# A fused attention + spiking-MLP layer: a sixth buffer for attention weights over the query/key planes, two pairs of value runs joined, and the places of an interval laid out anew

## The reference

```
xn = layernorm(x)
q, k, v = xn Wq + bq, xn Wk + bk, xn Wv + bv        # 16 heads of 16 features
q, k    = rotary(q), rotary(k)
attn    = softmax(causal(q k^T / 4)) v,  then  attn Wo + bo
h       = relu(xn W_fc)^2                            # 1024 features
y       = h W_proj                                   # 256 features
spikes  = 5 steps of: mem = 0.9 mem + y - (mem > 1); count (mem > 1);  count / 5
out     = x + attn part + spikes
```

## Time and profile before

| | us |
|---|---|
| runs, median of 3 | 2201.42 (2200.13 to 2207.49) |
| profiled execution | 2198.7 |
| its span, first to last instruction | 2196.9 |
| TensorE busy | 2093.1 (95% of the span) |
| ScalarE busy | 1451.5 (66%) |
| VectorE busy | 1403.9 (64%) |
| GpSimd busy | 1125.3 (51%) |

### The profile page before, as it was taken

How to read it: one execution, slowest core, us unless ns; L and a number is a source line. 1 busy time by engine, 2 the same in 40 slices (tenths; PEclk the granted TensorE clock), 3 DMA queues, 4 the chain that set the end, 5 groups by cost and what they waited for, 6 DMA issues and landing times.

```text
span 2196.9 us, 67675 instructions
## 1 busy us (share of the span) xinstructions
PE 2093.1 (95%) x25492; PEld 1502.4 (68%) x25492; DVE 1403.9 (64%) x2139; ACT 1451.5 (66%) x1676; POOL 1125.3 (51%) x1072
## 2 busy tenths in 40 slices
PE   5899999999999999999999999999999999999995
PEld 4667676767767677676767767677676766767663
DVE  7566585766758576585666757576585666757443
ACT  3666667666676766667666676766667667676662
POOL 5455473545646355463555646455463554636341
PEclk9999999999999999999999999999999999999997
DMA  5353635455364453635445364453635445364442
GB/s 198 118 157 87 192 104 156 138 118 181 93 183 112 127 173 87 197 104 151 143 116 179 94 177 116 127 175 86 199 104 150 144 111 180 97 172 120 111 113 70
DMA packets 169866, 299.97 MB, mean 137 GB/s; under 512 B 25104, under 2 KB 114960, under 8 KB 157200
## 3 DMA queue, kind: packets, MB, share of 16 engines
q1 hardware_dynamic: 169616, 296.10, 47.3%
HBM read 174.89 MB, written 103.28 MB: 127 GB/s over the span
## 4 chain that ended last, share of the span: by engine, by line
PE 64%; issue 11%; POOL 9%; DMA 6%; DVE 5%; ACT 3%; SPq 0%; POOLq 0%; DVEq 0%; ACTq 0%
PE pair L1525 17%; PE pair L1322 13%; PE pair L1508 10%; PE pair L1331 10%; PE pair L1300 6%; PE pair L1248 5%; DMA recip_rows<-recip_dram 4%; POOL probs L691 4%; POOL h_lo L683 3%; ACT probs L808 3%; PE pair L1314 2%; POOL rs L669 1%; DMA recip_dram<-denom 1%; DVE rs L1087 1%; DVE h_sq L1065 1%
## 5 line engine op out<-in xcount | busy, mean ns | idle before, releaser
L808 ACT ACTIVATE probs<-pair 128x1024 f32<-128x1024 f32 x1152 | 1146.2, 1029 | 552.9 <-PE pair L1508 552.0
L683 POOL TENSOR_TENSOR h_lo<-h_sq,h_hi 128x512 fp32r<-128x512 f32 x256 | 399.1, 1559 | 451.1 <-DVE h_hi L1067 450.7
L1331 PE MATMUL pair<-wproj_hi,h_hi 64*128 64x256 f32 x2048 | 584.8, 286 | 0.0
L691 POOL TENSOR_SCALAR_AFFINE_SELECT probs<-probs 128x512 f32<-128x512 f32 x512 | 395.3, 789 | 367.9 <-ACT probs L808 366.6
L1331 PE MATMUL pair<-wproj_hi,h_lo 64*128 64x256 f32 x2048 | 572.1, 279 | 0.0
L1331 PE MATMUL pair<-wproj_lo,h_hi 64*128 64x256 f32 x2048 | 571.7, 279 | 0.0
L1322 PE MATMUL pair<-xT_hi,wfc_hi 64*128 64x256 f32 x2048 | 546.6, 285 | 19.5 <-DVE y_sb L1094 8.2
L1525 PE MATMUL pair<-probs,v_sb 128*17 128x512 f32 (+3 forms) x6144 | 548.3, 488 | 13.3 <-POOL probs L691 12.5
L1322 PE MATMUL pair<-xT_lo,wfc_hi 64*128 64x256 f32 x2048 | 535.2, 279 | 0.0
L1322 PE MATMUL pair<-xT_hi,wfc_lo 64*128 64x256 f32 x2048 | 534.8, 279 | 0.0
L1508 PE MATMUL pair<-q_ring,k_ring 64*128 64x512 f32 (+3 forms) x3072 | 448.5, 359 | 18.3 <-ACT probs L808 14.6
(11 more groups left out here) (113 smaller groups left out, 2888.9 us busy)
## 6 DMA issues: line engine op xcount, KB each, us to landing
q_ring<-qk_dram SPq DMA_DIRECT2D x384, 128.0 KB
k_ring<-qk_dram SPq DMA_DIRECT2D x384, 128.0 KB
qk_dram<-planes SPq DMA_DIRECT2D x64, 512.0 KB, 2.8
qk_dram<-rot_b SPq DMA_DIRECT2D x62, 512.0 KB, 3.7
xn<-in_x SPq DMA_DIRECT2D x16, 1024.0 KB, 5.9
rs<-in_x SPq DMA_DIRECT2D x64, 256.0 KB, 2.9
acc_dram<-rs SPq DMA_DIRECT2D x64, 256.0 KB, 4.5
attn<-numer SPq DMA_DIRECT2D x256, 64.0 KB, 2.3
```

Of the source, the lines that this page charges most:

```text
L683: pool.tensor_tensor(h_lo[i % HB][:, :], h_sq[i % HB][:, :], h_hi[i % HB][:, :].bitcast(F32), ALU.subtract).then_inc(h_lo_done, 1)
L691: ins = pool.affine_select(view, view, [[0, 4], [1, P]], ALU.is_ge, 0.0, base=0, channel_multiplier=-1)
L808: act.activation(probs[BUFFER[n]][:, 2 * pr:2 * pr + 2, :], pair[m % NSLOT][:, :, :], ACT.Exp, scale=SCALE).then_inc(exp_done, 1)
L1331: return pe.matmul(proj_bank[:, t * D:(t + 1) * D], h[rows, a * T2 + t * P:a * T2 + (t + 1) * P], w[rows, f, :], start=i % ITEMS_OF_GROUP ...
```

## The change

There is a sixth weight buffer for four units of the second half (21, 26, 30 and 35), laid over the two `planes`; ScalarE waits for the stores of all planes before unit 21, and for all value runs of the interval before it writes plane 0. Units 13 to 19, and others, get other buffers. The runs of steps 12 and 13 become one at step 13, those of steps 16 and 17 one at step 17, so there are 14 runs. Nearly every table of places is new. The number of operations of each kind is the same. Cut only by the tables `STATS_AT` and `XN_AT` (statistics and normalisation on VectorE, spread over more places) and by context:

```diff
...
-RUNS = {2: ((0, 0), (1, 0), (1, 1), (2, 0)), 3: ((3, 0), (4, 0)), 4: ((5, 0), (5, 1), (6, 0)), 5: ((7, 0), (8, 0), (2, 1)),
-        6: ((9, 0), (10, 0), (10, 1), (11, 0)), 7: ((12, 0), (13, 0)), 8: ((14, 0), (14, 1), (15, 0)),
-        9: ((16, 0), (17, 0), (11, 1))}
-RUN_AT = {n + h * NSTEP // 2: [(u + 2 * NU * h, seg) for u, seg in run] for h in range(2) for n, run in RUNS.items()}
+EARLY_RUNS = {2: ((0, 0), (1, 0), (1, 1), (2, 0)), 3: ((3, 0), (4, 0)), 4: ((5, 0), (5, 1), (6, 0)),
+              5: ((7, 0), (8, 0), (2, 1)), 6: ((9, 0), (10, 0), (10, 1), (11, 0)), 7: ((12, 0), (13, 0)),
+              8: ((14, 0), (14, 1), (15, 0)), 9: ((16, 0), (17, 0), (11, 1))}
+LATE_RUNS = {11: EARLY_RUNS[2], 13: EARLY_RUNS[3] + EARLY_RUNS[4], 14: EARLY_RUNS[5], 15: EARLY_RUNS[6],
+             17: EARLY_RUNS[7] + EARLY_RUNS[8], 18: EARLY_RUNS[9]}
+RUN_AT = {**EARLY_RUNS, **{n: tuple((u + NUNIT // 2, seg) for u, seg in run) for n, run in LATE_RUNS.items()}}
-BUFFER = (0, 1, 2, 3, 4, 0, 1, 3, 4, 0, 1, 2, 3, 0, 1, 0, 3, 0, 1, 0, 2, 3, 4, 0, 1, 3, 4, 0, 1, 2, 3, 0, 1, 0, 3, 1)
+BUFFER = (0, 1, 2, 3, 4, 0, 1, 3, 4, 0, 1, 2, 3, 4, 0, 1, 3, 4, 0, 1, 2, 5, 3, 4, 0, 1, 5, 0, 3, 4, 5, 1, 2, 0, 3, 5)
+LATE_UNITS = [n for n in range(NUNIT) if BUFFER[n] == NPB - 1]
...
-VALUES_AT = {(0, 0): ((0, 0),), (0, 3): ((0, 1), (1, 0)), (1, 0): ((1, 1),), (1, 3): ((2, 0),), (1, 4): ((2, 1),)}
-TAKE_V_AT = {(0, 3): (0,), (1, 0): (1,), (1, 4): (2, 3)}
+VALUES_AT = {(0, 0): ((0, 0),), (0, 2): ((0, 1),), (0, 4): ((1, 0),), (1, 0): ((1, 1),), (1, 3): ((2, 0),),
+             (1, 4): ((2, 1),)}
+TAKE_V_AT = {(0, 2): (0,), (1, 0): (1,), (1, 4): (2, 3)}
-QK_AT = {(2, 4): (0, 0), (3, 1): (0, 1), (3, 3): (1, 0), (4, 0): (1, 1), (4, 3): (2, 0), (5, 0): (2, 1),
+QK_AT = {(2, 4): (0, 0), (3, 0): (0, 1), (3, 3): (1, 0), (4, 0): (1, 1), (4, 3): (2, 0), (5, 0): (2, 1),
          (5, 3): (3, 0), (6, 0): (3, 1)}
-SUM_QK_AT = {(3, 2): 0, (4, 2): 1, (5, 2): 2, (6, 2): 3}
-PLANE_AT = {(3, 4): 0, (4, 4): 1, (5, 4): 2, (6, 4): 3}
-SQUARE_AT = {(4, 2): 0, (5, 2): 1, (6, 2): 2, (7, 2): 3}
+SUM_QK_AT = {(3, 2): 0, (4, 1): 1, (5, 2): 2, (5, 4): 3}
+PLANE_AT = {(3, 4): 0, (5, 0): 1, (6, 0): 2, (7, 2): 3}
+SQUARE_AT = {(3, 4): 0, (5, 3): 1, (6, 2): 2, (7, 1): 3}
...
-MLP_AT = {(6, 3): (0,), (7, 0): (1,), (7, 4): (2,), (8, 2): (3, 4), (8, 4): (5, 6), (9, 3): (7, 8), (10, 0): (9,),
-          (10, 3): (10,), (11, 0): (11, 12), (11, 3): (13, 14), (12, 0): (15,), (12, 3): (16,), (13, 0): (17,),
-          (13, 3): (18,), (14, 0): (19, 20), (14, 3): (21, 22), (15, 0): (23,), (15, 3): (24,),
-          (16, 0): (25,), (16, 3): (26,), (17, 0): (27, 28), (17, 3): (29,)}
+MLP_AT = {(6, 4): (0,), (7, 0): (1,), (7, 4): (2,), (8, 2): (3, 4), (8, 4): (5,), (9, 2): (6,), (9, 4): (7, 8),
+          (10, 1): (9,), (10, 4): (10,), (11, 0): (11,), (11, 3): (12,), (11, 4): (13,), (12, 0): (14,),
+          (12, 2): (15,), (12, 3): (16,), (13, 0): (17,), (13, 3): (18,), (14, 0): (19,), (14, 2): (20,),
+          (14, 4): (21,), (15, 0): (22,), (15, 3): (23, 24), (16, 0): (25,), (16, 3): (26,), (16, 4): (27,),
+          (17, 0): (28,), (17, 4): (29,)}
-Y_AT = {(10, 0): 0, (13, 0): 1, (16, 0): 2}
+Y_AT = {(10, 2): 0, (13, 0): 1, (16, 0): 2}
-Y_CARRIED_AT = (1, 0)
+Y_CARRIED_AT = (2, 1)
...
-RELU_AT = {**expanded_at(MLP_AT, NFC), (7, 0): (0,), (7, 3): (1,)}
+RELU_AT = {(7, 0): (0,), (7, 2): (1,), (8, 2): (2,), (9, 0): (3,), (9, 4): (4,), (10, 4): (5,), (11, 0): (6,),
+           (11, 4): (7,), (12, 4): (8,), (13, 1): (9,), (14, 1): (10,), (14, 4): (11,), (15, 3): (12,),
+           (16, 0): (13,), (16, 4): (14,), (17, 4): (15,)}
...
-SPIKES_HERE = {(8, 3): (0, 0), (8, 4): (0, 1), (9, 1): (0, 2), (9, 2): (0, 3), (9, 3): (0, 4), (9, 4): (0, 5),
-               (10, 2): (1, 0), (10, 3): (1, 1), (10, 4): (1, 2), (11, 1): (1, 3), (11, 2): (1, 4), (11, 3): (1, 5)}
-SPIKES_NEXT = {(14, 1): (0, 0), (14, 2): (0, 1), (14, 3): (0, 2), (14, 4): (0, 3), (15, 1): (0, 4), (15, 2): (0, 5),
-               (15, 3): (1, 0), (15, 4): (1, 1), (16, 1): (1, 2), (16, 2): (1, 3), (16, 3): (1, 4), (17, 1): (1, 5)}
+SPIKES_HERE = {(8, 3): (0, 0), (8, 4): (0, 1), (9, 0): (0, 2), (9, 1): (0, 3), (9, 3): (0, 4), (10, 1): (0, 5),
+               (10, 3): (1, 0), (10, 4): (1, 1), (11, 2): (1, 2), (11, 3): (1, 3), (11, 4): (1, 4), (12, 3): (1, 5)}
+SPIKES_NEXT = {(13, 1): (0, 0), (13, 2): (0, 1), (13, 4): (0, 2), (14, 1): (0, 3), (14, 2): (0, 4), (14, 3): (0, 5),
+               (14, 4): (1, 0), (15, 1): (1, 1), (16, 3): (1, 2), (17, 0): (1, 3), (17, 2): (1, 4), (17, 4): (1, 5)}
-BIAS_HERE_AT, BIAS_NEXT_AT = {(8, 2): (0,), (10, 2): (1,)}, {(14, 2): (0,), (15, 4): (1,)}
-VAR_AT, ROOT_AT = (11, 4), (12, 0)
+BIAS_HERE_AT = {(7, 3): (0,), (10, 4): (1,)}
+BIAS_NEXT_AT = {(13, 0): (0,), (17, 0): (1,)}
+VAR_AT, ROOT_AT = (12, 1), (12, 4)
...
-        probs = [sb(f"probs{i}", [P, 4, G]) for i in range(NPB)]
+        probs = [sb(f"probs{i}", [P, 4, G]) for i in range(NPB - 1)]
+        planes_at = here()
         planes = [sb(f"planes{i}", [P, 2, G], F32R) for i in range(2)]
+        probs.append(over("probs_late", [P, 4, G], F32, planes_at))
...
-            def weigh(b, n, pr, last):
+            def weigh(b, n, pr, last, more):
                 before = BEFORE[n]
+                if n == LATE_UNITS[0] and pr == 0 and more:
+                    for s in planes_out:
+                        act.wait_ge(s, (b + 2) * 4 * 16)
                 if pr == 0 and (last or before >= 0):
...
                     if att and place != 2:
-                        weigh(b, 2 * n + place // 3, place % 3, last)
+                        weigh(b, 2 * n + place // 3, place % 3, last, more)
                     if more and at in PLANE_AT:
+                        if PLANE_AT[at] == 0 and (last or again):
+                            act.wait_ge(pv_done, (b + again) * NSEG)
                         plane_qk(nb, PLANE_AT[at])
```

More of the change, by code:

```diff
@@ L172 @@
 INVERT_LAST, DIVIDE_LAST, INVERT_AT, DIVIDE_AT = (1, 3), (3, 0), (11, 0), (14, 0)
-SPIKES_HERE = {(8, 3): (0, 0), (8, 4): (0, 1), (9, 1): (0, 2), (9, 2): (0, 3), (9, 3): (0, 4), (9, 4): (0, 5),
-               (10, 2): (1, 0), (10, 3): (1, 1), (10, 4): (1, 2), (11, 1): (1, 3), (11, 2): (1, 4), (11, 3): (1, 5)}
-SPIKES_NEXT = {(14, 1): (0, 0), (14, 2): (0, 1), (14, 3): (0, 2), (14, 4): (0, 3), (15, 1): (0, 4), (15, 2): (0, 5),
-               (15, 3): (1, 0), (15, 4): (1, 1), (16, 1): (1, 2), (16, 2): (1, 3), (16, 3): (1, 4), (17, 1): (1, 5)}
+SPIKES_HERE = {(8, 3): (0, 0), (8, 4): (0, 1), (9, 0): (0, 2), (9, 1): (0, 3), (9, 3): (0, 4), (10, 1): (0, 5),
+               (10, 3): (1, 0), (10, 4): (1, 1), (11, 2): (1, 2), (11, 3): (1, 3), (11, 4): (1, 4), (12, 3): (1, 5)}
+SPIKES_NEXT = {(13, 1): (0, 0), (13, 2): (0, 1), (13, 4): (0, 2), (14, 1): (0, 3), (14, 2): (0, 4), (14, 3): (0, 5),
+               (14, 4): (1, 0), (15, 1): (1, 1), (16, 3): (1, 2), (17, 0): (1, 3), (17, 2): (1, 4), (17, 4): (1, 5)}
 SPIKES_FINAL = {(16, 0): 0, (17, 0): 1}
-BIAS_HERE_AT, BIAS_NEXT_AT = {(8, 2): (0,), (10, 2): (1,)}, {(14, 2): (0,), (15, 4): (1,)}
-STATS_AT = {(10, 3): range(0, 4), (11, 4): range(4, 8)}
-VAR_AT, ROOT_AT = (11, 4), (12, 0)
-XN_AT = {(16, 4): range(0, 4), (17, 4): range(4, 8)}
+BIAS_HERE_AT = {(7, 3): (0,), (10, 4): (1,)}
+BIAS_NEXT_AT = {(13, 0): (0,), (17, 0): (1,)}
+STATS_AT = {(10, 1): (0,), (10, 2): (1, 2), (10, 3): (3,), (11, 0): (4,), (11, 1): (5,), (11, 3): (6,), (11, 4): (7,)}
+VAR_AT, ROOT_AT = (12, 1), (12, 4)
+XN_AT = {(16, 1): (0,), (16, 2): range(1, 4), (16, 3): (4,), (17, 0): (5,), (17, 2): (6, 7)}
 def spike_thresholds():
```

## The result

The changed kernel takes 2190.33 us (2188.13 to 2193.13, five runs) against 2201.42: a ratio of 0.9943, 95% interval 0.9927 to 0.996. That is the side forecast, with little over a third of the size: the forecast was 2171. The profiled execution took 2188.13 us, its span 2186.4.

What follows compares the result with a forecast made beforehand. TensorE's own queue was taken as the bound. Terms summed to -2.05 us per interval, -30.8 over 15 intervals, +0.8 in the last: profiled 2168.7, median forecast 2171 us (chance 0.55), range 2155 to 2193.

Steps and rivals of the forecast that it cites:

- Part 5: Step 8: item 1's ReLU, moved ahead of both exponentials on ScalarE, no longer delays the second score pair; -0.4 us per interval.
- Part 4: Steps 1 to 3: later y copy frees inversion, product moved, V copy earlier (0.15); -0.95 us per interval.
- Rival A: Steps 1 to 3: denominators come no earlier, because SyncE waits at the turn of the interval; 2181 us, chance 0.15.
- Part 2: Run of step 15: unit 29's mask ahead of item 11's ReLU on GpSimd removes the stall; -1.0 us per interval.
- Part 3: Steps 8 to 11: turn 10 waits less for the y copy, -0.4; turn 6's move nearly cancels; -0.35 us per interval.
- Part 1: Joined runs save 0.12 each, single score pairs between turns cost 0.29 each; with nothing waiting, 0.0 us per interval.
- Part 6: New waits: y copy uncovered at step 16, +0.5; turn 16 waits for item 7, +0.15; +0.65 us per interval.
- The last interval: Scores and exponentials alternate there and the run of step 16 loses its cover; +0.8 us, ends 0 and 1.8.
- B: Waits move rather than go: half the gain returns as small waits in steps 9 to 17; 2187 us, chance 0.15.
- C: Slower: item chains fall behind in steps 11 and 12, turn 16 waiting for item 7; 2209 us, chance 0.08.

Runs made afterwards that it cites:

- b2: The changed kernel with the two stores of plane 2 issued ahead of the 13 DMAs of the ring load; 2179.55 us, ratio 0.989 to the kernel before.
- a1: The changed kernel with item 1's ReLU at (7, 4) instead of (7, 2), behind both exponentials of step 7; 2183.3 us, ratio 0.9913 to the kernel before.
- b3: The kernel before with y copied at (2, 1), second query/key product at (3, 0), values and first copy at (0, 2) and (0, 4); 2189.09 us, ratio 0.9932.
- the repair alone: The kernel before with unit 29's masks ahead of item 11's low part on GpSimd and a bias moved to (13, 0); 2189.07 us, ratio 0.9938.
- c3: The changed kernel with sixteen runs, item 1's ReLU at (7, 4), item 5's at (10, 2), the kernel before's order from step 11 on; 2163.43 us, ratio 0.9821.
- c1: The kernel before with the edits of b3 and of the repair alone, and item 1's ReLU at (7, 4); 2169.96 us, ratio 0.9848.
- a2: The changed kernel with its two joined runs split again, so sixteen runs; 2185.71 us, ratio 0.992 to the kernel before.
- a4: The changed kernel with both halves of an item's turn put together at three places (steps 6, 12, 17); 2190.64 us, ratio 0.9947 to the kernel before.
- b1: The changed kernel with the edits of a1 and a2 together; 2174.54 us, ratio 0.987 to the kernel before.

## Why the prediction failed, step by step

- **Part 5, step 8: the step that failed.** "The store of the plane it waits for landed long before." It did not. Forecast -0.4, measured +0.25: 0.65 of the 1.47 missing per interval (-2.05 forecast, -0.58 measured). I had not looked at the store's queue. The trace of before had it: there too the stores stand behind the ring load, the second was issued at 1045.02 and landed 4.58 later, at 1049.60, after the exponential ahead of which the ReLU was to go had started (1049.28). Over its loop that landing comes 54.1 to 56.8 after the run of step 0, and in the kernel after the ReLU could have started at about 54.1. With the store early (b2) or the ReLU late (a1) the stretch gives 7.24 - 6.79 = 0.45, the forecast's size, and the ratio of b2 is 0.989, nearly twice the gain of the kernel after. The Trainium skill, Perfetto Trace Analysis, DMA Instruction — HWDGE (DVE, Sync), says that the profiled window of such an instruction ends before its data has moved. The trace agrees: 0.38 us in the timeline, 3.6 to 5.4 to landing. Before, SyncE's timeline and ScalarE's:

```profile
1045.02 0.38 SPq L427 DMA_DIRECT2D qk_dram<-rot_b  x1
```

```profile
1049.28 1.03 ACT L808 ACTIVATE probs<-pair 128x1024 f32<-128x1024 f32 x1 [0.92 <-PE pair L1508]
```

- **Part 4, steps 1 to 3: right but for the V copy.** Forecast -0.5 and -0.3 for step 3, measured -0.73 from step 2 to 4. Rival A is refuted: the gather moved by 0.73 us, not by 2 or more. The 0.15 of an earlier V copy did not come (+0.04 from step 0 to 2, and +0.05 in b3). That the split of a block of two value turns costs what the copy gives is my reading; neither was run by itself.
- **Part 2, step 15: right.** -1.0 forecast; the run itself lost 1.0, and the repair alone gives 0.80 per interval.
- **Part 3, steps 8 to 11: right.** -0.35 forecast, -0.32 measured; c3 against c1 gives 0.33 there. The parts came as forecast too: turn 10 stands 1.04 behind its two pairs, 0.56 over the scale where I took 0.65, and the two pairs ahead of the run of step 9 take 0.97 against 0.58 before, a wait of 0.39 where I took 0.25 to 0.35.
- **Part 1, order and joins: half right.** A joined run takes 3.56 against 1.84 + 1.84, the 0.12 forecast, but in place the joins bring nothing (a2). But 0.29 was one price for two things. A single pair between odd and even turn costs 0.23 + 1.44 - 1.43 = 0.24, between the two halves of an item's turn 0.34 + 1.51 - 1.43 = 0.42. The second kind also stands at step 6, which is most of the +0.15 from step 4 to 7 (a4 without it: 0.12 less).
- **Part 6, new waits: the y copy was right, turn 16 too small.** +0.5 for turn 26 (0.98 against 0.47); 0.67 - 0.23 = 0.44 for turn 16, not 0.15. From the end of its expansion (1336.22) to turn 16 item 7's chain takes 4.19, against 4.0 in my sum, and of the 0.3 by which that was late I had taken half. Its low part takes 1.67 beside a spike operation of VectorE, where I had taken half at 1.3.
- **Steps 11 to 17 as a whole** were to gain 0.35 (parts 2, 6 and 1), and gained nothing (+0.39, +0.06 and -0.45). Of that, 0.29 is turn 16's wait, above. c3 against b1 shows the new order dearer by 0.70 than the old one, of which turn 16's wait is 0.25 (0.59 there). How the rest divides among single pairs and small waits is not measured; in a4 mending places one by one moved the waits instead.
- **The last interval.** +0.8 for the cover of step 16, measured +1.1, so near by luck: in this execution the joined run of step 17 took 4.71 instead of 3.56. The window of that run in the kernel after shows the granted clock at 0.74 in the mean:

```profile
2147.40:2152.20 4.80, 4.80 (x42) 1.14 (x40) 3.89 (x7) 1.25 (x2) 0.00 (x0) 0.74 0.16 55
```

Less those 1.15 the stretch would be as long as before, by my estimate; one execution of each kernel cannot show more.

- **The range.** Added plainly, the ends that the parts name go from about -3.7 to about +1.1 per interval, not from -3.2 to -0.4. The measured -0.58 lies in either.

Of the rivals B (2187) comes closest in number, and a share of its mechanism is there: waits found again in steps 12 and 16. The largest loss was at step 8, outside the steps that it names. C did not occur: the chains keep up, at 0.44 for one turn.

## What to carry to other kernels

Before moving an instruction ahead of where it stood, look up for each semaphore it waits on when the event really comes: for a DMA that is the landing, with the DMAs that its queue has ahead of it, over many intervals and not in one. Repair the stalls one at a time, each alone on the kernel as it is: three edits of a few words gave 1.5%, where a new order with a sixth buffer gave 0.6% and hid its own losses. A run or any long block of the bounding engine that is taken out of the order was somebody's cover: list which copies and chains end under it.

## What the runs showed of the hardware

- The store of 512 KB that the ReLU waits for took 4.2 to 5.4 us to land in the 14 loop intervals of the kernel after, 5.3 in most, behind 13 DMAs of a ring load. In b2, ahead of them, it took 3.6 to 3.8. The place in the queue is not all: in the kernel before, behind the same 13, it took 3.6 to 3.7 in eight of 14 and 4.2 to 5.5 in the others. What makes the difference stays open.
- Two halves of one accumulation with a single score pair between them cost 0.18 more than two independent turns with the same pair between (turns 26 and 27 against 21 and 22 after). Put together at step 6 (a4) they gave back 0.12.
- The granted clock of TensorE in the last interval is not set by its program alone: the same program ran at 1.00 and at 0.57 at the same place, behind the same 1.64 busy of 3.00 us. From that interval's first run to the end one program took 147.3 after and 151.6 in b2, a difference as large as some of the edits bring. Loop intervals, at clock 1.00, are the safer measure.
